# Attention layer on one Trainium2 core: the softmax sums divided out in channel-major rows after a trip through DRAM

## The reference

```
n   = layernorm(x)
q, k = rope(n @ Wq.T), rope(n @ Wk.T);  v = n @ Wv.T        # 16 heads of 16 channels
att = softmax(q k.T / sqrt(16));  x = x + concat(att v) @ Wu.T + bu
n   = layernorm(x);  p = n shifted by one token
r   = sigmoid(mix(mu_r, n, p) @ W_r.T)
x   = x + r * (relu(mix(mu_k, n, p) @ W_k.T)^2 @ W_v.T)
```

## Time and profile before

| | us |
|---|---|
| median of 3 runs | 2461.25 (2447.2 to 2461.93) |
| the profiled execution | 2454.73 |
| its span, first to last instruction | 2452.9 |

### The profile page before, as it was taken

The page is one execution under the profiler, slowest core; times in us unless marked ns, Lnnn a source line. Parts: engine busy times, 40 slices in busy tenths (PEclk is TensorE's granted clock), DMA queues, the critical chain, the costliest instruction groups (busy, mean ns, idle before and its releaser), DMA issues.

```text
span 2452.9 us, 48193 instructions
## 1 busy us (share of the span) xinstructions
PE 2258.4 (92%) x13084; PEld 1192.8 (49%) x13084; DVE 2036.2 (83%) x3982; ACT 1644.1 (67%) x3073; POOL 1391.3 (57%) x1184
## 2 busy tenths in 40 slices
PE   5899999999999999999999999999999999999995
PEld 3445444555455455444455444455545545554443
DVE  5788888889888888888888888888888988997762
ACT  2467767667677676767667777676767776776653
POOL 5336665556665455666555665555666655566224
PEclk8789999999999999999999999999999999999877
DMA  6433455543455543454543355553345554334400
GB/s 152 95 86 95 91 108 115 120 98 90 83 103 120 121 101 89 94 108 103 120 108 91 85 107 103 120 121 90 94 87 104 120 121 109 92 100 79 94 27 22
DMA packets 133559, 243.09 MB, mean 99 GB/s; under 512 B 24848, under 2 KB 79760, under 8 KB 120976
## 3 DMA queue, kind: packets, MB, share of 16 engines
q1 hardware_dynamic: 133264, 239.56, 44.3%
HBM read 136.71 MB, written 83.89 MB: 90 GB/s over the span
## 4 chain that ended last, share of the span: by engine, by line
PE 58%; DVE 12%; issue 10%; DMA 10%; SPq 5%; ACT 3%; DVEq 1%; POOL 1%; ACTq 0%; POOLq 0%
PE d_ps L957 23%; PE st_ps L895 16%; PE pv_ps L927 11%; DMA q_st<-mparts 9%; PE s_ps L913 7%; DVE mx L693 5%; SPq L325 5%; PE d_ps L951 2%; DVE xrT L792 2%; ACT probs L652 1%; ACT parts L585 1%; DVE ynT L719 1%; DVE mparts L706 1%; PE d_ps L943 1%; DVE stats L749 1%
## 5 line engine op out<-in xcount | busy, mean ns | idle before, releaser
L652 ACT ACTIVATE probs<-st_ps 128x512 f32<-128x512 f32 x2048 | 1153.8, 597 | 702.5 <-PE st_ps L895 693.9
L693 DVE TENSOR_REDUCE mx<-s_ps 128x1 f32<-128x512 f32 x2048 | 1341.7, 679 | 327.0 <-PE s_ps L913 321.5
L895 PE MATMUL st_ps<-q_st,k_st 50*128 50x512 f32 x2048 | 820.1, 465 | 96.6 <-DMA q_st<-mparts 47.2
L913 PE MATMUL s_ps<-k_st,q_st 48*128 48x512 f32 x2048 | 865.9, 483 | 46.3 <-DVE mx L693 38.5
L895 PEld LDWEIGHTS st_ps<-q_st,k_st 50*128 50x128 f32 x2048 | 333.6, 190 | 616.2 <-ACT probs L652 324.0
L927 PE MATMUL pv_ps<-probs,v_ext 128*32 128x512 f32 x4096 | 563.9, 623 | 0.0
L913 PEld LDWEIGHTS s_ps<-k_st,q_st 48*128 48x128 f32 x2048 | 352.0, 190 | 127.0 <-DVE mx L693 105.2
L473 POOL TENSOR_TENSOR rs<-ve,mhalf 128x2 f32<-128x2 f32 x128 | 89.7, 701 | 435.9 <-DVE mean L761 435.9
L465 POOL TENSOR_TENSOR f_lo<-yn,f_hi 128x512 fp32r<-128x512 f32 x128 | 164.2, 1293 | 115.5 <-ACT f_hi L620 115.5
L458 POOL TENSOR_TENSOR f_lo<-attnT,f_hi 128x512 fp32r<-128x512 f32 x64 | 86.9, 1358 | 200.4 <-ACT f_hi L608 200.3
L435 POOL TENSOR_TENSOR parts<-parts 128x1024 fp32r<-128x1024 f32 x62 | 147.4, 2377 | 65.8 <-ACT parts L585 65.8
(11 more groups left out here) (118 smaller groups left out, 3962.6 us busy)
## 6 DMA issues: line engine op xcount, KB each, us to landing
parts_scratch<-parts SPq DMA_DIRECT2D x64, 1024.0 KB, 5.1
q_st<-parts_scratch SPq DMA_DIRECT2D x128, 256.0 KB, 6.4
k_st<-parts_scratch SPq DMA_DIRECT2D x128, 256.0 KB, 7.4
xn<-in_L_attn_x_dram SPq DMA_DIRECT2D x32, 512.0 KB, 5.9
q_st<-parts_scratch SPq DMA_DIRECT2D x128, 128.0 KB, 7.8
k_st<-parts_scratch SPq DMA_DIRECT2D x128, 128.0 KB, 8.1
attnT<-attn SPq DMA_DIRECT2D x512, 32.0 KB, 2.0
y<-in_L_attn_x_dram SPq DMA_DIRECT2D x32, 512.0 KB, 8.9
```

The source lines that it names most:

```text
L652: nc.scalar.activation(probs[:, u % SLOTS, j, :], st_ps[:, n % 2, :], ACT.Exp, scale=float(D) ** -0.5).then_inc(exp_done, 1)
L693: nc.vector.tensor_reduce(mx[:, col:col + 1], s_ps[:, n % 2, :], AX.X, ALU.max).then_inc(max_done, 1)
L895: nc.tensor.matmul(st_ps[:, n % 2, :], k_st[par][row:row + SROWS + MROWS, slot, c * P:(c + 1) * P], q_st[par][row:row + SROWS + MROWS, slo ...
L913: nc.tensor.matmul(s_ps[:, n % 2, :], q_st[at][row:row + SROWS, slot, qc * P:(qc + 1) * P], k_st[at][row:row + SROWS, slot, :], start=True ...
```

## The change

- The sums are no longer divided out in token blocks. ScalarE copies each group's `pv_ps` bank into a new tile `raw` (`raw_evac`, four per step, at (1, 0), (5, 1), (9, 1) and (13, 0)), and SP stores it to DRAM (`store_raw`, 256 KB each).
- `load_att(s, o)` waits until two groups are stored and reads them back twice: the 16 channel rows of 8 heads into the 128 rows of `attnT[:, o]`, and the 8 rows of sums, each repeated 16 times, into `sumT`. VectorE then does one reciprocal and one product of 128x512 (`invert`, `normalise`): for o = 0 at (13, 1) and (14, 2), for o = 1 in the next step at (2, 2) and (2, 3).
- VectorE loses both transposes, the small reciprocal and the small product of each group.
- `row_max_T` moves from the end of its unit to just behind the dense work of the same unit, and the `split_max` halves move to earlier slots: M1 from (2, 1), (2, 2) to (1, 3), (2, 0); M2 from (6, 0), (6, 1) to (5, 3), (6, 0); M3 from (10, 1), (10, 2) to (9, 2), (9, 3); M0 from (14, 1), (14, 2) to (13, 2), (13, 3).
- `high`, one copy of 128x1024 at (11, 1) and at (15, 2), becomes two of 128x512 at (11, 1), (11, 2) and at (15, 1), (15, 3).
- SP's order is new: `store_parts` now comes first, and the second half of `load_stacks` comes after `move_max(b, 2)` as before but `load_x` and `store_raw(b, 0)` before it.
- The rows of Wu are loaded in another order, to fit the new order of channels.

```diff
-                def normalise(s, g, stage):        # transpose, reciprocal of 128x16, product of 128x256, transpose
...
+                def invert(s, o):
+                    if s.active():
+                        dve.wait_ge(att_in, s.count(64, 32 * (o + 1)))
+                        nc.vector.reciprocal(sumT, sumT).then_inc(inverted, 1)
+                def normalise(s, o):
+                    if s.active():
+                        dve.wait_ge(inverted, s.count(2, o + 1))
+                        nc.vector.tensor_tensor(attnT[:, o, :], attnT[:, o, :], sumT, ALU.mult).then_inc(att_norm, 1)
...
+                def raw_evac(s, g):
+                    if s.active():
+                        act.wait_ge(pv_done, s.count(UNITS, TC * (g + 1)))
+                        if s.has(16 * NG, 16 * g):
+                            act.wait_ge(raw_out, s.count(16 * NG, 16 * g))
+                        nc.scalar.activation(raw[:, :], pv_ps[:, g % 2, :], ACT.Copy).then_inc(raw_done, 1)
...
+                def load_att(s, o):
...
+                    sp.wait_ge(raw_out, s.count(16 * NG, 32 * (o + 1)))
...
+                    sp.dma_start(attnT[:, o, :],
+                                 bass.AP(rows.tensor, rows.offset, [[32 * T, 8], [T, D], [1, T]])).then_inc(att_in, 16)
+                    sp.dma_start(sumT, bass.AP(rows.tensor, rows.offset + D * T,
+                                               [[32 * T, 8], [0, D], [1, T]])).then_inc(att_in, 16)
...
-                move_attn(b.plus(-1), 3)
+                store_parts(b.plus(1), 1 - par, 1)
+                store_raw(b.plus(-1), 3)
+                load_att(b.plus(-1), 1)
                 move_max(b, 1)
                 store_out()
-                store_parts(b.plus(1), 1 - par, 1)
                 load_stacks(0)
+                load_x()
+                store_raw(b, 0)
                 move_max(b, 2)
-                load_x()
                 load_stacks(1)
-                move_attn(b, 0)
                 load_residual()
+                store_raw(b, 1)
                 move_max(b, 3)
-                move_attn(b, 1)
+                load_att(b, 0)
+                store_raw(b, 2)
                 move_max(b.plus(1), 0)
-                move_attn(b, 2)
                 store_parts(b.plus(2), par, 0)
```

More of the change, by code:

```diff
@@ L121, in layer_kernel @@
         mparts = sb("mparts", [GH * TC, MROWS, P], F32R)
-        inv = sb("inv", [P, T // 32])
-        attn = sb("attn", [P, T])
+        raw = sb("raw", [P, T])
         attnT = sb("attnT", [P, CB, T])
@@ L129, in layer_kernel @@
         ynT = sb("ynT", [P, CB, T + 1])
-        sums = ynT[:, 0, 1:T + 1]
+        sumT = ynT[:, 0, 1:T + 1]
         stats2 = sb("stats2", [P, TC, 6])
@@ L302, in load_stacks, with store_raw @@
                                          src).then_inc((stack_in, stack2_in)[go], 16)
-                def move_attn(s, g):
+                def store_raw(s, g):
                     if not s.active():
                         return
-                    sp.wait_ge(attn_done, s.count(4, g + 1))
+                    sp.wait_ge(raw_done, s.count(NG, g + 1))
                     carry_wait(b)
[L309 to L315, removed]
+                    if g == 0 and s.plus(-2).has(64, 64):
+                        sp.wait_ge(att_in, s.plus(-2).count(64, 64))
+                    sp.dma_start(raw_rows[s.add % 2, g], raw[:, :]).then_inc(raw_out, 16)
+                def load_att(s, o):
+                    if not s.active():
+                        return
+                    sp.wait_ge(raw_out, s.count(16 * NG, 32 * (o + 1)))
+                    carry_wait(b)
+                    if s.plus(-1).has(2, o + 1):
+                        sp.wait_ge(a_lo_done, s.plus(-1).count(2, o + 1))
+                        carry_wait(b)
+                    if o == 1:
+                        sp.wait_ge(att_norm, s.count(2, 1))
+                    elif s.plus(-1).has(4, 4):
+                        sp.wait_ge(shift_done, s.plus(-1).count(4, 4))
+                    rows = raw_rows[s.add % 2, 2 * o]
+                    sp.dma_start(attnT[:, o, :],
+                                 bass.AP(rows.tensor, rows.offset, [[32 * T, 8], [T, D], [1, T]])).then_inc(att_in, 16)
+                    sp.dma_start(sumT, bass.AP(rows.tensor, rows.offset + D * T,
+                                               [[32 * T, 8], [0, D], [1, T]])).then_inc(att_in, 16)
                 def move_max(s, g):
@@ L550, in yT_evac @@
                             act.wait_ge(shift_done, s.plus(-1).count(4, 4))
-                        if b.has(NG, 1):
-                            act.wait_ge(attn_done, b.count(NG, 1))
+                        act.wait_ge(att_norm, s.count(2, 2))
                         nc.scalar.activation(ynT[:, n, 1:T + 1], d_ps[:, BANK["YT", n], :], ACT.Copy).then_inc(ynT_done, 1)
@@ L830, in step @@
                 extras = {(0, 0): [(gate_v, b.plus(-2), 0)], (0, 3): [(gate_v, b.plus(-2), 1)],
-                          (1, 0): [(normalise, prev, 3, 0)], (1, 1): [(normalise, prev, 3, 1)],
-                          (1, 3): [(normalise, prev, 3, 2)],
-                          (2, 1): [(split_max, b, 1, 0)], (2, 2): [(split_max, b, 1, 1)],
+                          (1, 3): [(split_max, b, 1, 0)], (2, 0): [(split_max, b, 1, 1)],
+                          (2, 2): [(invert, prev, 1)], (2, 3): [(normalise, prev, 1)],
@@ L834, in step @@
+                          (13, 1): [(invert, b, 0)], (14, 2): [(normalise, b, 0)],
                           (3, 3): [(split_xnT, 0)], (4, 0): [(split_xnT, 1)], (4, 3): [(residual, 0)],
-                          (5, 0): [(stats2_of, 0, 0)], (5, 1): [(stats2_of, 0, 1)], (5, 3): [(residual, 1)],
-                          (6, 0): [(split_max, b, 2, 0)], (6, 1): [(split_max, b, 2, 1)],
+                          (5, 0): [(stats2_of, 0, 0)], (5, 1): [(stats2_of, 0, 1)], (5, 3): [(residual, 1), (split_max, b, 2, 0)],
@@ L843, in step @@
+                          (10, 0): [(shift, 1, 1)],
                           (10, 3): [(shift, 0, 0)], (11, 2): [(shift, 0, 1)],
[L844 to L847, removed]
-                          (15, 0): [(normalise, b, 2, 0)], (15, 1): [(normalise, b, 2, 1)],
@@ L922, in values @@
                         pe.wait_ge(v_done, s.count(2, 2))
-                    if c == 0 and s.has(3 * NG, 3 * g - 5):
-                        pe.wait_ge(norm_step, s.count(3 * NG, 3 * g - 5))
+                    if c == 0 and s.has(NG, g - 1):
+                        pe.wait_ge(raw_done, s.count(NG, g - 1))
                     for j in range(GH):
```

69 lines of the change are left out of this document (25 added, 44 removed).

## The result

The changed kernel takes 2693.5 us (median of 4 runs, 2678.4 to 2697.9), the kernel before 2456.0: a ratio of 1.0945, 95% interval 1.0912 to 1.0979. The prediction was 2538, its range ended at 2615. The sign was right, the size was not: the change costs 237 us, where I had 80 to 85.

A forecast was written before the change was run, and what follows sets the result against it. TensorE held 58% of the chain; moving waits could bring at most 4 to 5% of the step. Per step -3.5 + 4.0 + 1.2 + 0.8 = +2.5 us, times 32 = 80, +4 at the end: 2538 us, range 2395 to 2615.

The forecast's parts named there:

- The clock: A 4 us TensorE stall in u3 should bring the lower granted clock in many steps: 0.8 us per step, between 0 and 1.5.
- the loop's edge: At the hardware loop's edge every second u0 takes some 3 us more, with granted clock 0.50 behind it; forecast to stay.
- The price in slot (13, 1): The invert at (13, 1), its data in time, lies beside the dense work and costs 1.2 us per step.
- The reciprocal, R: VectorE's reciprocal of 128x512 takes 2.8 us, 2.6 to 3.4 in the main case.
- The trip: w: VectorE waits at (2, 2) for the load out of DRAM: 1.5 us, between 0.5 and 2.5.
- The gains: Waits taken away: 1.8 us at u8 with the knock-on in u9, 0.5 in u0, 1.2 in u2; 3.5 per step.
- The bound of 4 to 5%: The most of a step that moving waits can bring while TensorE does the same work, not 15%.
- The streaming reciprocal: Rival: reciprocal takes 0.74 us, stall at u3 1.9, nothing at u13, no clock falls; 2406 us (2380 to 2435), chance 0.26.
- The stalls did not hide in each other: Rival: stalls overlap at the loop's edge, u0, u1 and u12, some 2 us per step of cost go; 2460 us, chance 0.11.
- The late trip with a longer divide: Rival: wait 3.5 and reciprocal 4.0 us, +7.5 us per step, 2699 us; decides from a sum above 5.5; chance 0.06.
- M2 was cured: Rival said M2's DMA still lands behind the stacks: 1.8 us per step back, +58 us; counted inside the other cases.

The follow-up runs named there:

- without the reciprocals: The changed kernel with the division left out, channel rows multiplied by the sums themselves, both invert slots still waiting for their loads: 2491.6 us, ratio 1.0138.
- without the trip: The changed kernel with the second half's load reading rows of input x, issued ahead of the store, in place of the stored rows: 2591.5 us, ratio 1.0555.
- without either: The changed kernel without its reciprocals and with the second half's load reading input x in place of the stored rows: 2357.2 us, ratio 0.9572.
- the run with 16: The changed kernel with its two loads written with 16 as slowest DRAM dimension in place of 8, same bytes: 2643.2 us, ratio 1.0732.
- the fastest version: The kernel before with high in halves, SP's new order, row_max_T and M1 to M3 early, M0 in old slots, GpSimd's add_bu behind low_a(1): 2343.2 us, ratio 0.9537.

## Why the prediction was right in sign and wrong in size

**The clock: the step that failed.** "A stall of 4 us in u3 should bring the same in many steps. I take 0.8, between 0 and 1.5." The row behind it, the loop's edge, had 1.4, and a stall of 4 us was forecast for every step; the stall in u14 got no low clock at all. The traces give, per step over the same steps as the unit lengths, for how long TensorE has no matmul in flight, and for how long it works while the granted clock is 0.50:

| | whole step | idle | at work at 0.50 |
|---|---|---|---|
| before | 72.8 | 4.1 | 3.1 |
| changed | 81.0 | 8.6 | 10.5 |
| without the reciprocals | 74.4 | 4.4 | 6.5 |
| without the trip | 77.2 | 6.4 | 6.4 |
| without either | 70.1 | 2.5 | 1.3 |

Between the last version and the changed kernel lie 10.9 us of time, but only 6.1 of idle time. The other 4.8 is work that takes longer, and 9.2 us more of it are done at 0.50. By units it is 2.0 us in u3 and 0.8 in u4, against a quiet 3.5 and 4.2; of their work 3.7 and 2.3 us are done at 0.50. In u14 some 0.8 is an estimate: without the trip the same reciprocal stands in the same slot, u14 has 0.3 us at 0.50 and takes 6.3, where it has 2.1 at 0.50 and takes 7.1 in the changed kernel. That makes 3.6 us; in the rest of the 4.8 TensorE may also have been held to the pace of VectorE's maxima. No run sets the clock alone, so its share is an estimate by differences, but 0.8, or 1.5, is ruled out by u3 and u4. The clock did not follow the stall's length either: an idle time of 1.9 us in u3 (without the reciprocals) brought 2.2 us of slower work in u3 and u4, and one of 4.9 brought 2.8.

**The price in slot (13, 1): the second step that failed.** "The nearest row is unit 1 of before ... I take 1.2." Measured 2.9: some 0.8 of it the low clock as above, and 2.1 the slot itself. The term had no range, and no clock was put on it. Unit 1 of before had about the same sum of work, but in pieces between which row maxima ran. With the work in four pieces, spread over three units, u14 costs nothing, and u15 and u0 1.2 together.

**The reciprocal, R.** "I take 2.8, as 14 streamed values would explain only 14 of the 72 ns." That it isn't streamed was right, and so the sign. But I took a fixed part of 161 ns from another instruction. The three widths measured lie on one line: 233 ns at 16, 942 at 128, 3350 at 512, which is 6.3 ns per value and a fixed part of some 130. So R = 3.35 and not 2.8. At 0.96 GHz, the clock that the Trainium skill gives for VectorE ("VectorE: DVE Perf Modes", Specifications), 6.3 ns is an estimated 6 cycles; the 8 that I read out of its repeat count is not what the chip took.

**The trip: w.** I had VectorE wait 1.5 us. In the steps of the loop it waited 2.1 on the mean; the total of 79.7 us in 34 waits holds two of 6.5 and 8.9 at the end of the program. The store landed in 2.0 us or, where it was issued close behind `store_parts`, in 2.4 to 3.5, against my 2.5. The load of the sums' rows took 4.7 to 5.3 us after its issue, where I had 4.4 from a least landing of 3.5. The eight-row shape is worth some 1.2 us of that, as the run with 16 showed. I had that rule on the page and left it as an end of the range; the trace of before had no row for it.

R and w are both off, but inside their ranges. With the two as measured and 0.5 in place of the 0.3 that is covered, the stall is 4.95 in place of 4.0; with every other term as it stood the sum would give some 2570 us, inside the range. They alone did not put the result outside.

**The sum of the costs.** 4.0 + 1.2 + 0.8 = 6.0 us per step were forecast; 10.9 were found when both causes were taken away: 4.9 of idle TensorE in u3, some 2.1 in the slot at u14, some 3.6 of low clock behind the two, and 0.3 that I can't place. With the 0.8 us of gains below that did not come, 5.7 us per step were missing, 182 us in 32 full steps. The gap between 2538 and 2693 is 155; the first and the last steps hold less of the work.

**The gains.** 3.5 us per step were forecast, 2.7 found in the version with neither cost. u2 gave 1.1 (1.2 forecast) and u0 0.6 (0.5). u8 gave 1.0 and not 1.65, because I took the length of u3, 3.54, for its quiet length; it is 4.17 in all versions whose M2 is in time. The mechanism was right, SP's order more than the slots. That the removed 10.6 us on VectorE bring nothing by themselves fits too, though no run takes them away alone: with all of it in place, the last versions keep u7, u13 and u15 within 0.35 us of a quiet unit. The bound of 4 to 5% on what moving waits can bring was badly put: by the lengths given there the quiet units sum to 14 x 4.17 + 2 x 3.54 = 65.5 us and not 66.5, so 7.4 us of the 72.86 are waits, 10%. It is 4 to 5% only with the loop's edge and u12 left out, and the fastest version took 4.6% without touching the edge.

**The rivals.** The streaming reciprocal is ruled out by 3350 ns. The stalls did not hide in each other: u12 even rose from 5.22 to 5.73. The late trip with a longer divide stood at 2699 with a chance of 0.06. Its time was met, but not its condition: w = 2.1 and R = 3.35 are below its 3.5 and 4.0, and their sum of 5.45 is below its point of 5.5. That it names the right time is luck, as the clock made up what the waits did not have. M2 was cured.

**What I did not see coming.** GpSimd in the chain. The statistics of the norm moved from (14, 0) to (14, 3), GpSimd works in order, and its `rope_sums` and with them `high` at (15, 1) wait behind the scales: ScalarE waited 59.4 us in 30 times for it, 15.5 of them once. u15 holds 0.35 us more than before (4.52), and the same without reciprocal and trip (4.55), while it is 3.96 in the kernel before with `high` in halves and the statistics where they were. That points to the statistics, but no run moves them alone.

## What to carry to other kernels

Cost a new operation by its length in one piece and by the slot in which it stands, not by what it takes off the engine's busy sum: this change took 10.6 us of VectorE's work per step away, put 8.1 back and lost 8.3. To each stall of TensorE add the slower work behind it as a term of its own, read from a row in which the granted clock is low; here that was 2 to 3 us for the stall in u3, more than was wrong with the wait and the divide together. A fixed part and a rate need two widths of the same operation; one width with the fixed part of another instruction gives neither. And price an order of transfers on a queue as its own change: SP's order alone was worth 2.2%, where the early slots alone lost 1.2% and on top of SP's order brought some 0.5%, with overlapping intervals.

## What the runs showed that I had not expected

- The reciprocal on VectorE costs 6.3 ns per value: 233 ns, 942 ns and 3350 ns for 16, 128 and 512 values per partition, where a product of 512 takes 684.
- TensorE's low clock behind a stall cost nearly as much for a short one as for a long one: 2.2 us of slower work in u3 and u4 behind 1.9 us of idle time, 2.5 behind 2.7, 3.1 behind 3.8, 2.8 behind 4.9.
- Writing the slowest DRAM dimension as 16 in place of 8 took the landing of a 256 KB load from 4.7 to 5.3 us down to 3.8 to 4.1, with the same bytes, and the share of busy DMA engines from 0.52 up to 0.99.
- A 2.39 us addition on GpSimd, started just before a VectorE product of 0.43 us, made that product 2.0 us long. Moving one line was worth 1.6% of the kernel.
- A reciprocal cut in four took 0.42 us more of VectorE and 44 us less of the kernel.
